# Attention maxima from two 64-row halves of the array, reduced by one VectorE pass over two PSUM banks

## What is computed

```python
x = x + _L0_xattn_ref(_layernorm(x), ctx_512, ...)        # x (8, 256, 256), ctx (8, 1601, 64)
q_hk = (hidden_q @ Wq.T).reshape(Bv, Sv, H, K)             # H = 16 heads, K = 128
q_big = einsum('bshk,hkq->bshq', q_hk, w_kc_q)             # 192 wide, then rope
kv_r = _apply_rope(kv_c, sin_k, cos_k)                     # 64 wide, shared by the heads
scores = einsum('bhsr,bhlr->bhsl', q_r, k_r)               # (q W_qr)(kv W_kr)^T
attn = softmax(scores, axis=-1)                            # over 1601 context rows
ctx_c = einsum('bhsl,bld->bhsd', attn, kv_r)
...                                                        # w_kc_kv and Wo
```

## Time and profile before

| | |
|---|---|
| time, median of 3 runs | 1769.66 us (1766.52 to 1771.66) |
| the profiled execution, its time | 1781.06 us |
| its span, first to last instruction | 1779.2 us |
| mean granted clock of TensorE | 0.96 of full |
| PE busy | 1653.8 us (93%), 16216 matmuls |
| DVE busy | 1328.9 us (75%), 2910 instructions |
| ACT busy | 1015.1 us (57%) |
| POOL busy | 925.9 us (52%) |
| DMA | 144.14 MB, mean 81 GB/s |

### The profile page before, as it was taken

One profiled execution on the slowest core, in us unless ns is written; L12 is line 12 of the kernel. 1 busy time (PEld: TensorE's weight loads), 2 busy tenths in 40 slices (PEclk: granted clock), 3 DMA queues, 4 the chain that ended last, 5 costly groups with the idle time before them and its releaser, 6 DMA issues. The chain is left out here.

```text
span 1779.2 us, 48732 instructions
## 1 busy us (share of the span) xinstructions
PE 1653.8 (93%) x16216; PEld 1326.5 (75%) x16216; DVE 1328.9 (75%) x2910; ACT 1015.1 (57%) x2028; POOL 925.9 (52%) x623
## 2 busy tenths in 40 slices
PE   5789999999999999999999999989777799987898
PEld 4568888888888888888888888868655455557776
DVE  5788888888888888888888888886564378874223
ACT  5676666666666666666666666652122266662111
POOL 5337777777777777777777777760002122111321
PEclk8699999999999999999999999999988899997999
DMA  9621121221221121121121142139300000004244
GB/s 261 232 80 51 58 85 50 58 81 50 61 77 53 57 83 52 58 83 52 55 83 53 52 128 79 56 98 315 92 11 23 21 13 12 12 7 172 93 140 146
DMA packets 150154, 144.14 MB, mean 81 GB/s; under 512 B 41306, under 2 KB 137224, under 8 KB 149600
## 3 DMA queue, kind: packets, MB, share of 16 engines
q1 hardware_dynamic: 148432, 139.56, 25.9%
q0 software_dynamic: 1536, 3.99, 0.6%
q10 hardware_dynamic: 144, 0.07, 0.0%
HBM read 91.61 MB, written 33.98 MB: 71 GB/s over the span
## 5 line engine op out<-in xcount | busy, mean ns | idle before, releaser
L1152 POOL TENSOR_TENSOR c_rest<-c_prob 128x1024 f16<-128x1024 f32 (+1 forms) x513 | 796.4, 1573 | 310.9 <-ACT c_prob L947 297.0
L947 ACT ACTIVATE c_prob<-c_psS,ln,c_exp_scale 128x1024 f32<-128x1024 f32 (+1 forms) x514 | 538.1, 1047 | 239.8 <-PE c_psS L783 234.7
L1053 DVE TENSOR_REDUCE c_mxp<-c_psM 128x1 f32<-128x400 f32 (+1 forms) x1040 | 589.4, 573 | 111.2 <-PE c_psM L767 97.0
L783 PE MATMUL c_psS<-c_q,c_kk 128*128 128x256 f16 (+1 forms) x3350 | 512.7, 273 | 0.2 <-issue 0.2
L801 PE MATMUL c_psV<-c_vb,c_prob 128*128 128x129 f16 (+1 forms) x3328 | 396.3, 222 | 0.0
L783 PEld LDWEIGHTS c_psS<-c_q,c_kk 128*128 128x128 f16 (+1 forms) x3350 | 321.9, 99 | 85.7 <-issue 0.4
L804 PE MATMUL c_psV<-c_vb,c_rest 128*128 128x65 f16 (+1 forms) x3328 | 374.1, 193 | 0.0
L767 PE MATMUL c_psM<-c_kkm,c_q 128*128 128x400 f16 (+1 forms) x1040 | 346.1, 333 | 4.8 <-DVE c_mxp L1053 3.0
L804 PEld LDWEIGHTS c_psV<-c_vb,c_rest 128*128 128x128 f16 (+1 forms) x3328 | 301.2, 99 | 22.1
L801 PEld LDWEIGHTS c_psV<-c_vb,c_prob 128*128 128x128 bf16 (+1 forms) x3328 | 305.2, 97 | 14.0
L729 PE MATMUL c_psQ<-c_xb,c_w2s 128*128 128x256 f16 x1188 | 164.1, 275 | 11.6 <-PEq L162 9.9
(11 more groups left out here) (298 smaller groups left out, 2153.6 us busy)
## 6 DMA issues: line engine op xcount, KB each, us to landing
c_w2s<-w_scr SPq DMA_DIRECT2D x66, 256.0 KB, 2.6
acc_scr<-c_acc SPq DMA_DIRECT2D x128, 129.0 KB, 2.2
c_ms<-m_scr SPq DMA_DIRECT2D x67, 192.0 KB, 2.3
c_w2s<-w_scr SPq DMA_DIRECT2D x66, 128.0 KB, 2.1
kv<-acc_scr SPq DMA_DIRECT2D x4, 2064.0 KB, 9.8
d_acc<-acc_scr SPq DMA_DIRECT2D x4, 2064.0 KB, 8.6
m_w<-in_L_ffn_W SPq DMA_DIRECT2D x16, 352.0 KB, 4.2
c_vb<-V SPq DMA_DIRECT2D x27, 129.0 KB, 2.0
```

What stands on the lines that cost most here:

```text
L783: mm = pe.matmul(psS[g % 2][0:r, i * S:(i + 1) * S], src[:, (lo + i) * P:(lo + i) * P + r], mov[slot][:, :], start=(one == 0 and i % 2 == ...
L947: nc.scalar.activation(prob[g][0:r, 0:w], psS[g % 2][0:r, 0:w], ACT.Exp, bias=keep["ln1024"][0:r, :], scale=exp_scale[slot][0:r, :]).then_ ...
L1053: nc.vector.tensor_reduce(mxp[:, st, c:c + 1], psM[:, st, 0:CHUNKS[c][1]], AX.X, ALU.max).then_inc(mx_done, 1)
L1152: nc.gpsimd.tensor_tensor(rest[g][0:r, 0:w], prob[g][0:r, 0:w], high[0:r, 0:w], ALU.subtract).then_inc(rest_done, 1)
```

## The change

In the first attention:
- The maxima use the high part of the context alone. Both row halves of `kkm` now hold the high rows of `KK1` (two DMAs a chunk, each half the size). For a chunk c two matmuls are issued one behind the other: row block 0 with array rows 0 to 63 into bank 0, row block 1 with rows 64 to 127 into bank 1. There are 4 passes a head instead of 8, and pass c waits for reduction c-1.
- DVE reduces both banks in one instruction (4 a head).
- `mx` and `shiftT` move from `psM` to the second bank of `psS[1]`; `join` now waits for the exp of group 1 of the head before, and `scores(n, 0)` for `shift_copy`.
- The bodies of PE, DVE and ACT are written in a new order, different for even and odd heads; the last maxima pass of head n+1 is done in body n where n is even; `q_other` moves behind the drain of `psV`; in the prologue `psK` has one buffer in `psV` instead of in `psS[1]`'s second bank.
- `wvo` stays in SBUF.

In the preparation: the store of `wvo` is dropped, ScalarE's square root for the layer norm comes after head 3 instead of 7, the first `turn_context` on DVE goes ahead of the norm bound, the key scale ahead of the wait for the bound, and the load of the exp table goes from the attention's prologue to the end of the preparation.

```diff
@@ preparation
-    wvo = sb("a_wvo", [P, H0 // 2, D])
+    wvo = keep["wvo_made"]
...
-            sp.wait_ge(vo_done, N_VO)
-            sp.dma_start(t["wvo_scr"], wvo[:]).then_inc(stored, 16)
             sp.wait_ge(keep["in_wA"], 16)
             sp.wait_ge(keep["in_wR"], 16)
-            sp.wait_ge(stored, 16 * 2)
+            sp.wait_ge(stored, 16)
...
-                if h == H0 // 2 - 1:
+                if h == 3:
                     act.wait_ge(var_ready, 1)
...
+            nc.scalar.activation(warm[:], eps[:], ACT.Exp)
...
+            turn_context(POOL_TURNS)
             n = D_NM
             dve.wait_ge(d_full, n + 1)
@@ first attention
-    PASSES = 2 * len(CHUNKS)
+    PASSES = len(CHUNKS)
...
-    shiftT = psM[0:ST * 2 * SHIFT_ROWS, 1, SPARE:SPARE + P // 2].bitcast(F16)
-    mx = psM[:, 1, SPARE + P // 2:SPARE + P // 2 + ST]
+    shiftT = psS[1][0:ST * 2 * SHIFT_ROWS, 512:512 + P // 2].bitcast(F16)
+    mx = psS[1][:, 512 + P // 2:512 + P // 2 + ST]
...
         c0, w = CHUNKS[c]
-        queue.dma_start(kkm[:, c0:c0 + w], KK1[:, bass.ds(b * L + c0, w)]).then_inc(in_kkm[c], 16)
+        for half in range(2):
+            queue.dma_start(kkm[half * DC:(half + 1) * DC, c0:c0 + w],
+                            KK1[DC:P, bass.ds(b * L + c0, w)]).then_inc(in_kkm[c], 16)
...
-            def maxima(n, p, k, slot):
-
-                c, st = divmod(k, ST)
-                if k == 0:
+            def maxima(n, p, c, slot):
+
+                if c == 0:
                     pe.wait_ge(qh_done, 4 * p + 4)
-                if k == 1 and not (isinstance(n, int) and n == 0):
-                    pe.wait_ge(shift_done, n)
-                if not (isinstance(n, int) and n == 0 and k < ST):
-                    pe.wait_ge(mx_done, PASSES * n + k - 1)
+                if not (isinstance(n, int) and n == 0 and c == 0):
+                    pe.wait_ge(mx_done, PASSES * n + c)
                 c0, w = CHUNKS[c]
-                pe.matmul(psM[:, st, 0:w], q1[slot][:, st * P:(st + 1) * P], kkm[:, c0:c0 + w],
-                          start=True, stop=True).then_inc(mx_full, 1)
+                for st in range(ST):
+                    rows = slice(st * DC, (st + 1) * DC)
+                    mm = pe.matmul(psM[:, st, 0:w], q1[slot][rows, st * P:(st + 1) * P], kkm[rows, c0:c0 + w],
+                                   start=True, stop=True)
+                mm.then_inc(mx_full, 1)
...
                 if k0 == 0:
                     pe.wait_ge(exp_done, 4 * n + g + 1)
+                    if g == 0:
+                        pe.wait_ge(shift_done, n + 1)
...
+                        q_second(p)
+                        maxima(n + 2, p2, 0, s2)
+                        values(n, 0, (0, 2))
+                        scores(n, 3, u)
+                        values(n, 0, (2, 3), shift_of=n + 1)
+                        shift(n + 1)
...
@@ ACT
+                    if u % 2 == 1:
+                        q_other((AHEAD // 2) * j + (AHEAD + u) // 2, u - 1)
@@ DVE
-            def reduce_max(n, k):
-                c, st = divmod(k, ST)
-                dve.wait_ge(mx_full, PASSES * n + k + 1)
...
-                nc.vector.tensor_reduce(mxp[:, st, c:c + 1], psM[:, st, 0:CHUNKS[c][1]], AX.X,
-                                        ALU.max).then_inc(mx_done, 1)
+            def reduce_max(n, c):
+                dve.wait_ge(mx_full, PASSES * n + c + 1)
...
+                nc.vector.tensor_reduce(mxp[:, :, c], psM[:, :, 0:CHUNKS[c][1]], AX.X, ALU.max).then_inc(mx_done, 1)
...
             def join(n):
                 dve.wait_ge(mx_done, PASSES * (n + 1))
+                if not isinstance(n, int) or n > 0:
+                    dve.wait_ge(exp_done, 4 * n)
```

More of the change, by code:

```diff
@@ L705, in _ @@
                 sp.wait_ge(sent[u], 16 + 16 * (H0 // 2))
-            sp.dma_start(keep["wvo"], t["wvo_scr"]).then_inc(keep["in_wvo"], 16)
+            sp.dma_start(keep["wvo"], keep["wvo_made"][:]).then_inc(keep["in_wvo"], 16)
             sp.dma_start(keep["acc0"].rearrange("p h s w -> p h (s w)"),
@@ L723, in _, with q_rows @@
         def _(pe):
-            def q_rows(out, weights, maxima_of=None):
+            def q_rows(out, weights):
                 for c in range(DK):
                     for i, (w, x) in enumerate(((0, 0), (0, 1), (1, 0))):
-                        if maxima_of is not None and c == DK - 1 and i == 2:
-                            pe.wait_ge(mcol_done, 2 * maxima_of + 2)
                         mm = pe.matmul(out, weights[:, w, c], xb[:, x, c, :],
@@ L866, in _ @@
             scores(0, 0, 0)
+            maxima(1, 0, 1, 1)
+            q_lat(1)
             maxima(1, 0, 2, 1)
-            maxima(1, 0, 3, 1)
-            q_lat(1)
-            maxima(1, 0, 4, 1)
             pe.wait_ge(k1_done, 16)
             scores(0, 1, 0)
-            maxima(1, 0, 5, 1)
-            maxima(1, 0, 6, 1)
-            maxima(1, 0, 7, 1)
-            scores(0, 2, 0, (0, 6))
+            scores(0, 2, 0, (0, 4))
             with pe.Fori(0, N // AHEAD) as j:
@@ new lines, in _ @@
+                        values(n, 1, (0, 1))
+                        maxima(n + 2, p2, 1, s2)
+                        values(n, 1, (1, 3))
+                        scores(n + 1, 0, s1)
+                        scores(n + 1, 1, s1, (0, 6))
+                        maxima(n + 2, p2, 2, s2)
+                        values(n, 1, (3, 4))
+                        scores(n + 1, 1, s1, (6, 8))
+                        values(n, 2, (0, 2))
+                        scores(n + 1, 2, s1)
+                        maxima(n + 2, p2, 3, s2)
@@ new lines, in _ @@
+                        values(n, 2, (2, 4))
+                        values(n, 3)
+                    else:
+                        q_second(p)
+                        maxima(n + 2, p2, 0, s2)
+                        values(n, 0, (0, 2))
+                        scores(n, 3, u)
+                        values(n, 0, (2, 3), shift_of=n + 1)
+                        shift(n + 1)
+                        values(n, 0, (3, 4))
+                        values(n, 1, (0, 3))
+                        maxima(n + 2, p2, 1, s2)
+                        values(n, 1, (3, 4))
+                        scores(n + 1, 0, s1)
+                        values(n, 2, (0, 1))
+                        q_lat(p)
+                        maxima(n + 2, p2, 2, s2)
+                        scores(n + 1, 1, s1, (0, 2))
+                        values(n, 2, (1, 2))
+                        scores(n + 1, 1, s1, (2, 8))
+                        values(n, 2, (2, 3))
+                        scores(n + 1, 2, s1, (0, 2))
+                        values(n, 2, (3, 4))
+                        scores(n + 1, 2, s1, (2, 4))
+                        values(n, 3)
@@ L1112, in _ @@
             scale_of(1, 1)
+            v_rest(7)
             turn_second(1)
@@ L1115, in _ @@
             add_second(1)
-            for k in range(PASSES):
-                reduce_max(1, k)
+            reduce_max(1, 0)
+            reduce_max(1, 1)
+            reduce_max(1, 2)
             q_low(1, 2)
```

168 lines of the change are left out of this document (70 added, 98 removed).

## The result

| | before | after |
|---|---|---|
| time, median | 1769.30 us (1766.52 to 1771.66, 4 runs) | 1791.79 us (1789.38 to 1794.64, 4 runs) |
| the profiled execution: time, span | 1781.06, 1779.2 us | 1789.38, 1787.3 us |
| first attention's first shift transpose | 104.94 us | 98.62 us |
| second | 115.64 us | 108.02 us |
| last | 1186.6 us | 1206.0 us |

The changed kernel takes 1.0123 times as long (95% interval 1.0109 to 1.0136), 22.5 us more. The last three lines of the table say where it went: the prologue ends 7.6 us earlier, then 127 heads take 27.0 us longer, (1206.0 - 108.02) against (1186.6 - 115.64). That leaves 19.4 us at the last shift transpose. Behind it the code is unchanged.

A forecast was written before the change was run, and what follows sets the result against it. PE was taken to bound the kernel. Maxima +27, new waits +2, preparation -5 and prologue -1 make +23: the profiled 1781.06 becomes 1804, and as it lies 0.6% over the median, 1793 us, range 1776 to 1832.

The forecast's parts named there:

- What bounds: First attention's loop: PE waits for nobody, stalls at most 0.1 us per pair of heads, so savings on other engines earn nothing.
- Maxima on PE, +27: Four visits a head to the half-height form at 0.39 us each, against 0.338 for the two matmuls replaced: +27 us.
- drain: PE's wait when the array changes form; put at 0.09 us in the chain from one maxima pass to the next.
- Weights in the open: Second attention's score product L1870: first records 104 ns longer (693 against 589) because fp32 weights load in the open.
- The new waits, +2: Single maxima buffer: chain of 1.52 us against PE's 1.57, and ScalarE's copy 4.2 against 4.3; both hold, put at +2.
- rival A: Maxima visits nearly free in fp16, under 0.33 us each; kernel faster, about 1700 us; chance 0.11.
- The loop, +29: First attention's loop, +27 for the maxima and +2 for waits; a pair of heads named as 17.27 us instead of 16.9.
- VectorE, 0: Joint reductions of 0.99 us cut VectorE by 0.63 us a head, to 77% busy; not the bound, so 0 earned.
- Preparation, -5 and -1: Dropped `wvo` store and earlier context turn start the attention at 76.8 us: -5; prologue up to the loop: -1.
- The sum: Whole kernel: +27 + 2 - 5 - 1 = +23, giving 1793 us.
- B: Rival: weights load in the open as in fp32, 0.48 us a maxima visit, 1837 us; chance 0.10.
- C: Rival of no difference: a maxima visit of 0.345 us and all of the preparation's gain, 1768 us; chance 0.06.

The follow-up runs named there:

- e4: The kernel before with each of its eight maxima matmuls a head on array rows 64 to 127 alone, nothing else changed: 1988.53 us.
- e2: The changed kernel with both maxima matmuls of a visit on array rows 0 to 63: 1875.17 us.
- e1: The changed kernel with the maxima in the full 128-row form again, new order, single buffer and preparation kept: 1786.31 us.
- e7: The changed kernel with VectorE's wait for the next `kkm` refill put ahead of its wait for the maxima: 1787.19 us.
- e8: e1 with VectorE's wait for the next `kkm` refill put ahead of its wait for the maxima: 1771.33 us.
- e6: The kernel before with all of the new preparation and the exp table loaded there, its attention loop untouched: 1767.59 us.

## Why the prediction was right

Predicted were 1793 us (1776 to 1832) and "slower" with 0.82; the measurement is 1791.79. Step by step:

- **What bounds.** PE, and nothing beside it. Right for the load: DVE lost 12.9 us in 200 and nothing came of it. But the changed kernel waits for VectorE at two places, 0.08 us a pair in all (below).
- **Maxima on PE, +27.** Right in mechanism, a little high in size. A visit was put at 0.39 us against 0.338. Measured are 0.096 at the entry (0.205 from a score's start where 0.109 would do), 0.003 to the second start, 0.272 to the next matmul, and about 0.01 in that one's weights (613.39 to 613.46 is 0.07, 0.06 for its successors): 0.38. So it is 0.043 above the old cost, not 0.052, and 8 x 64 x 0.043 = 22 us, not 27. e4 confirms the price of a visit, 0.210, and e2 that the halves run at once. The entry and the exit together take 0.20 to 0.21, and running two matmuls of 400 columns at once gives back 0.166 of it.
- **What the prediction calls a drain.** Measured is a late start: 0.10 us ahead of each L764, and with the exit 0.210 a visit in e4. What the array does in that time no run shows. Two halves at once save 0.160 a visit against one half twice (e2), but a whole visit of two matmuls of 400 columns takes 0.38 us in the changed kernel, more than the 0.338 of two in the full form.
- **Weights in the open.** The prediction puts the 104 ns of L1870's first records down to them. The trace of the kernel before shows it: the weight loads of the first two records start with these, at 1498.10, 0.18 us long; those of the other two start at 1498.21, well ahead of their records at 1498.64. Over the whole phase 92 records whose load starts with them take 693 ns and 92 with the load ahead 589, of 196. The fp32 product L752 of the changed kernel has both cases as well, 483 and 379 ns. In fp16 the difference is about 0.01 us: a visit's first L764 in e2, whose load starts with it, takes 339 ns, the second, with the load ahead, 329.
- **The new waits, +2.** This is the step that failed, and another error hid it. The sum "0.09 drain + 0.37 from matmul to reduction + 0.99 + about 0.07 back = 1.52" took 0.37 from a reduction that has no arithmetic for a second wait to pass. At the fourth pass it is 0.55. The 0.09 does not belong there: the maxima start 0.05 to 0.06 behind the end of the reduction in either form (616.67 to 616.72 in the changed kernel, 614.24 to 614.30 in e1). So the chain is 1.60, not 1.52, against PE's 1.56, and the place does not hold "by 0.05 to 0.1" but misses by 0.037 (the maxima start 0.242 behind the last q matmul, 0.205 in e7). The forecast puts the rope's wait at nothing (only rival A has one): `q_lat` waits 0.044 for the rope in the changed kernel, and no longer in e7. Together that is 0.081 a pair, 5 us in the changed kernel. The other place named as thin, ScalarE's copy, held: the maxima behind it start 0.205 after a score in the changed kernel and 0.109 in e8, as without a wait.
- **The loop, +29.** Eight visits of 0.043 and the 0.081 are 0.425 us a pair; measured are 0.426 (17.29 against 16.87), +27.3 over 64 pairs. The visits were put 5 us too high and the waits 3 too low, so that the errors largely cancelled, which is luck. The 17.27 a pair that the prediction names does not follow from its own sum: +29 on 16.87 is 17.32. That it lies near 17.29 proves nothing.
- **VectorE, 0.** Right. 0.99 us for 800 elements was right too, and the lengths of VectorE's records add up to 0.66 us less a head, forecast was 0.63. Its busy share is 80%, not 77%: before, neighbouring reductions overlapped by about 0.1 (two in 1.06 us), so that the busy time counted them short.
- **Preparation, -5 and -1.** The attention starts at 75.70, predicted was 76.8, a gain of 6.1 instead of 5. From there to the second shift it takes 32.3 us, before 33.8: -1.5. The delay for the weights behind SP's four more DMAs came, 0.66 us. With the old loop (e6) the same edits brought the first shift 4.4 us forward and the median 3.7 us: one step of the prologue ran there at the lower clock, 1.4 us longer.
- **The sum.** +27.0 - 7.6 = +19.4 at the last shift, +22.5 by the medians. Some 2 to 3 us of the difference may lie in the four runs of the kernel before: their median is 1769.3, and 1771.2 to 1771.9 in the 43 runs beside most of the experiments. Against those the change costs 20 us, as the trace has it. The forecast of +23 had the preparation 1.6 us too weak and the loop 2 us too dear, 3.6 over the trace's 19.4 in all; that it meets the 22.5 of the medians within half a microsecond is luck. Its range has a slip too: the upper end takes -3 for the preparation with the prologue, where its own bounds (-3 and +3) make 0. Nothing hangs on it.
- **The rivals.** A (visits nearly free) would have shown a start 0.109 behind a score; it was 0.205. B (0.48 a visit) fell too: 0.38 was measured, with about 0.01 in the weights. C needed 0.345 a visit.

## What to carry to other kernels

Two half-height matmuls side by side between full-height work paid a price here to enter and leave the form, 0.21 us a visit, the same for one matmul of 400 columns (e4) as for two at once (after); count visits, and look for a place in the kernel's own trace that already changes form to read the price. An experiment that undoes one cost of a busy engine can lengthen a chain that the engine then waits for (e1, 0.24 us a pair at one place): read the waits in its trace, and mend them too, before judging the first cost. Where a chain between two engines is short of slack, put the wait that is met early, with the arithmetic for its value, ahead of the one that is met last, so that nothing stands between the late one and the work; here that gave 5 us (e7) and 15 us (e8).

## What of the hardware was not expected

- Register arithmetic of 0.115 us for a wait that is long met, left behind the decisive wait, makes the reduction start 0.16 us later (0.53 against 0.37 in e1 and e8, 0.55 against 0.38 after and in e7). The same wait without the arithmetic (the other three passes, 0.37 in e1 and 0.38 after where VectorE is waiting already) costs nothing that shows.
- The price does not follow the work around it: entry 0.096 and exit 0.103 are the same after scores of 256 columns, after value matmuls of 65 and after the fp32 product, and for one matmul in the form (e4) as for two (after).
- The prologue's granted clock rises at different times: from 84 to 90 us it is 0.50 before, 0.58 in e6 and 1.00 after, and the same products take 2.93 us in e6 and 1.56 after. It is small here, and its cause stays open.
